# A value-and-output projection kernel: the first load in two halves by partitions, and four clips moved behind two casts

## The reference

```
q = cond @ Wq.T + bq;  k = x @ Wk.T + bk;  v = x @ Wv.T + bv
scores = q . k / sqrt(32) per head           # one number for each row of x and head
context = clip(scores, 0, 1) * v             # per head
out = x + context @ Wo.T + bo
```

## Time and profile before

| what | value |
|---|---|
| median of 3 runs | 178.35 us (177.8 to 178.4) |
| the profiled execution | 178.37 us |
| its span, first to last instruction | 176.5 us |
| TensorE busy | 171.7 us, 97% |
| VectorE busy | 158.1 us, 90% |
| ScalarE busy | 110.9 us, 63% |
| granted TensorE clock | 1.000 of full |
| transfers | 29.72 MB, 168 GB/s mean |

### The profile page before, as it was taken

One profiled execution on the slowest core, in us unless ns is written; L12 is line 12 of the kernel. 1 busy time (PEld: TensorE's weight loads), 2 busy tenths in 40 slices (PEclk: granted clock), 3 DMA queues, 4 the chain that ended last, 5 costly groups with the idle time before them and its releaser, 6 DMA issues.

```text
span 176.5 us, 2441 instructions
## 1 busy us (share of the span) xinstructions
PE 171.7 (97%) x859; PEld 134.7 (76%) x859; DVE 158.1 (90%) x163; ACT 110.9 (63%) x150; POOL 10.7 (6%) x16
## 2 busy tenths in 40 slices
PE   8899999999999899999999999999999999999993
PEld 2786857687788688888688888888688888888883
DVE  0798499989988899989998899999999999999963
ACT  3658697974588857583489765766299555684300
POOL 0000000000000020111000010111000010111000
PEclk9999999999999999999999999999999999999999
DMA  5999950079900589998006844297107024197544
GB/s 199 368 348 419 418 202 0 0 207 425 400 15 0 155 322 378 323 195 133 17 0 193 297 97 97 19 187 122 35 17 197 0 22 97 18 169 114 178 178 178
DMA packets 7307, 29.72 MB, mean 168 GB/s; under 512 B 1088, under 2 KB 1472, under 8 KB 6976
## 3 DMA queue, kind: packets, MB, share of 16 engines
q1 hardware_dynamic: 5568, 23.29, 36.2%
q0 software_dynamic: 1728, 6.29, 21.2%
HBM read 19.61 MB, written 14.68 MB: 194 GB/s over the span
## 4 chain that ended last, share of the span: by engine, by line
PE 95%; DMA 2%; issue 1%; ACT 0%; DVE 0%
PE bank_y L327 10%; PE bank_y L329 10%; PE bank_y L331 10%; PE bank_x L327 8%; PE bank_x L331 8%; PE bank_x L329 8%; PE bank_z L327 6%; PE bank_z L329 6%; PE bank_z L331 6%; PE bank_x L412 5%; PE score_bank L395 4%; PE bank_z L412 3%; DMA work<-first_t 2%; PE bank_x L430 2%; PE bank_y L430 2%; PE bank_y L412 2%
## 5 line engine op out<-in xcount | busy, mean ns | idle before, releaser
L553 ACT CAST form_hi<-work 128x1024 fp32r<-128x1024 f32 x28 | 28.9, 1053 | 16.6 <-DVE work L841 7.0
L796 DVE TENSOR_TENSOR form_lo<-work,form_hi 128x1024 fp32r<-128x1024 f32 (+1 forms) x30 | 35.0, 1185 | 2.5 <-ACT form_hi L553 2.5
L589 ACT ACTIVATE work<-bank_y,const 128x512 f32<-128x512 f32 x30 | 20.2, 688 | 14.7 <-PE bank_y L331 14.6
L327 PE MATMUL bank_x<-form_hi,wo_hi 128*128 128x512 f32 x52 | 20.4, 392 | 0.6 <-issue 0.6
L589 ACT ACTIVATE work<-bank_x,const 128x512 f32<-128x512 f32 x24 | 16.3, 688 | 6.7 <-PE bank_x L331 6.5
L331 PE MATMUL bank_x<-form_hi,wo_lo 128*128 128x512 f32 x52 | 20.3, 390 | 0.0
L329 PE MATMUL bank_x<-form_lo,wo_hi 128*128 128x512 f32 x52 | 20.2, 389 | 0.0
L782 POOL DMA_DIRECT2D out_t<-work x12 | 10.5, 875 | 149.8 <-DVE work L823 143.0
L812 DVE SCALAR_TENSOR_TENSOR work<-relu,work 128x1024 f32<-128x1024 f32 x16 | 19.3, 1219 | 0.0
L327 PE MATMUL bank_y<-form_hi,wv_hi 128*128 128x512 f32 x48 | 19.0, 397 | 0.0
L796 DVE TENSOR_TENSOR form_lo<-x_home,form_hi 128x1024 fp32r<-128x1024 f32 x15 | 18.3, 1219 | 0.6 <-ACT form_hi L620 0.6
(11 more groups left out here) (133 smaller groups left out, 343.3 us busy)
## 6 DMA issues: line engine op xcount, KB each, us to landing
x_home<-x_t SPq DMA_DIRECT2D x16, 512.0 KB, 7.0
out_t<-x_t SPq DMA_DIRECT2D x12, 512.0 KB, 8.3
out_t<-work POOLq DMA_DIRECT2D x12, 512.0 KB, 5.4
relu<-relu SPq DMA_DIRECT2D x12, 128.0 KB, 2.3
work<-first_t SPq DMA_DIRECT2D x2, 512.0 KB, 3.9
work<-wq_t SPq DMA_DIRECT2D x2, 512.0 KB, 8.9
work<-wk_t SPq DMA_DIRECT2D x2, 512.0 KB, 11.3
work<-wo_t SPq DMA_DIRECT2D x1, 1024.0 KB, 15.2
```

Of the source, the lines that this page charges most:

```text
L327: pe.matmul(bank[:, j, :], hi, form_hi[:, kind, k, :], start=k == 0 and not grows, stop=False, skip_group_check=grows)
L553: nc.scalar.copy(flat(form_hi, kind), raw(kind, phase)).then_inc(hi_ready[kind], 1)
L589: nc.scalar.activation(result_set(phase)[:, q, j * ROWS:(j + 1) * ROWS], of[:, j, :], ACT.Identity, bias=bias[:, tile:tile + 1], scale=sca ...
L796: return nc.vector.tensor_tensor(to, of, hi.bitcast(F32), ALU.subtract)
```

## The change

The load of the first tile (k = 0) is issued as two transfers of 64 partitions each: partitions 0 to 63 by SyncE, partitions 64 to 127 by ScalarE, as the first thing in ScalarE's list. Both raise `first_loaded[0]`, and all who wait for it now wait for 32. The load for k = 1 stays whole and SyncE's. Apart from that, `clip_scores(1)` is moved down in ScalarE's list past `hi(T2, 2)` and `hi(B22, 2)`.

```diff
+FIRST_LOADS = (2 * 16, 16)
...
-            for k in range(2):
-                sp.dma_start(work[1][:, k, :], first_t[k]).then_inc(first_loaded[k], 16)
+            sp.dma_start(work[1][0:P // 2, 0, :], first_t[0, 0:P // 2, :]).then_inc(first_loaded[0], 16)
+            sp.dma_start(work[1][:, 1, :], first_t[1]).then_inc(first_loaded[1], 16)
...
             def first_half(k, semaphore):
-                act.wait_ge(first_loaded[k], 16)
+                act.wait_ge(first_loaded[k], FIRST_LOADS[k])
...
+            act.dma_start(work[1][P // 2:P, 0, :], first_t[0, P // 2:P, :]).then_inc(first_loaded[0], 16)
             first_half(0, first_half_hi)
...
             hi(B11, 3)
-            clip_scores(1)
             hi(T2, 2)
             hi(B22, 2)
+            clip_scores(1)
             hi(B21, 3)
```

More of the change, by code:

```diff
@@ L941, in first_w_hi @@
             def first_w_hi(form, k):
-                dve.wait_ge(first_loaded[k], 16)
+                dve.wait_ge(first_loaded[k], FIRST_LOADS[k])
                 nc.vector.tensor_copy(wv_hi[:, form, k, :], first_w[form][:, k, :]).then_inc(wv_hi_ready[form], 1)
```

## The result

Over 22 runs the changed kernel has a median of 178.58 us (178.08 to 180.55), the kernel before 178.42 us (177.8 to 179.04) over as many. The ratio of after to before is 1.0044, 95% interval 1.0025 to 1.0063: a little slower. The medians hide what happened. The kernel before has one group of runs. The changed kernel has two: 12 of its 22 runs lie from 178.08 to 178.66, mean 178.36, and 10 from 179.76 to 180.55, mean 180.20. None of the 22 lies under the lowest run of the kernel before. The profiled execution is of the upper group, 180.55 us with a span of 178.7.

The account below looks back on a forecast made before the run. TensorE, busy for 97% of the span, was taken to bound the kernel. From 178.37 us, 0 for the split load and −0.71 for the moved clips gave 177.7 us, range 177.2 to 178.6.

Parts of the forecast that it names:

- The clips: ScalarE, phase 2: clips hold the cast of T2 for 1.2 us; moving them gains 0.71 us, at most 0.84.
- VectorE's add: VectorE, phase 2: this add, at 56.94, precedes T2's lo part, which would start at 58.08 instead of 58.79.
- the cast of T3: ScalarE, phase 2: ends at 62.4 instead of 62.23; 1.4 us of cover before TensorE needs T3's lo part, cost nothing.
- The margin at T2 of phase 4: Narrowest gap after the stall between a lo part's end and its product: 1.6 us, so the whole 0.71 should last.
- The first load: Kernel start: splitting it into partition halves was priced at 0, with 0.21 us won at best and 1.09 lost at worst.
- inner range of ±0.2: Kernel start: expected change of the first tile's landing, −0.2 to +0.2 us around 0, assuming something near the full rate.
- the bad end: Kernel start: both halves move at 221 GB/s throughout, so the first tile takes 2.37 us instead of 1.28, 1.09 later.
- the 221 GB/s of the spread: Rate of the clips' spreading over 32 partitions while alone, where full tiles moved 410; taken as the low-rate bound.
- My bound of +1.09: Kernel start: largest delay in us forecast for the first tile's landing, with both halves at 221 GB/s all through.
- The half-rate rival: Kernel start: halves move like the 32-partition spread or one starts an issue later; costs 0.2 to 1.09 us, 178.2 us; chance 0.26.
- The table load: ScalarE's start: forecast to move from 0.73 to about 1.2 at no cost; rival with it ahead: 178.9 us, chance 0.05.
- a later landing: Kernel start: a landing later or earlier by d moves TensorE's start by d, and nearly all follows to the end.

Follow-up runs that it names:

- the larger set of runs: Clips moved, first load whole on SyncE, against the kernel before, run a second time: median 177.70 us over 12 runs, ratio 0.9961; means 0.82 us apart.

## Why the prediction was wrong

The prediction was 177.7 us, 0.4% faster, with a range of 177.2 to 178.6. The median of 178.58 lies at its very edge, and the time moved the other way.

**The clips: right, by its mechanism and its size.** The stall was the clips' doing, and 0.71 us was forecast; the trace of this edit alone shows 0.72, and the larger set of runs 0.8. VectorE's add is the next thing late, as said. What was left is 0.04 us there and 0.08 in the changed kernel; the 0.08 by which T2's second matmul follows late stayed (59.09 to 59.40), so 0.76 and not 0.84 was the most to be had. Of the pushed work, the cast of T3 was forecast to leave 1.4 us of cover, and it leaves 1.4 (66.53 to 67.97). The margin at T2 of phase 4 stayed at 1.6, since VectorE moved along with TensorE.

**The first load: wrong, and this is the step that failed.** I took 0 with an inner range of ±0.2, on the ground that with both halves under way at once the other half fills in. It does not. TensorE's first product started 0.8 us later in one profile of the changed kernel and 1.5 in the other. The row that I had set as the bad end, the 221 GB/s of the spread, was the nearer one: 229 to 283 GB/s while halves are being moved. My bound of +1.09 was too small for two of the four profiles with a half in each queue: the last half landed at 5.02, 5.24, 5.53 and 5.74 instead of 4.24, so 0.8 to 1.5 us late. At the mean rates up to the landing, 210 GB/s against 299, the 0.82 MB of the kernel before would take 3.9 us instead of 2.74; this estimate gives 1.2 of the 1.5 us of the profiled run. One term that was not in the bound is the issue: a half's takes 0.57 and not 0.21 or 0.43, with or without a second queue. What the rest is made of isn't shown. The half-rate rival, to which I gave 0.26 and 178.2 us, is what happened, and at the upper end of its price or above. The table load did move behind the new issue, to 1.33, and costs nothing, as forecast.

**What I did not price at all: the clock.** I passed a later landing on to TensorE's start one to one. In 10 of 22 runs it came with 1.7 to 1.8 us more (the trace, and the two groups' means), as the idle before the first product grew from 0.5 to 1.75 us and the first eight matmuls ran at 1.2 GHz. The cover here is the nine warm-ups, and the trace of before had them in it. I had named what hides each edit, but not what the warm-ups hide. For the profiled run the terms are 178.37 + 1.5 (start) + 1.7 (clock) − 0.7 (T2) = 180.9, measured 180.55; 0.3 of the rest lies between the eleventh product and the last of B21, 51.55 us in this profile (10.57 to 62.12) and 51.83 in that of before (7.40 to 59.23). For the lower group, 178.38 (mean before) + 0.8 − 0.7 = 178.5, measured 178.36, with the 0.8 from a single profile of another set. That the median came so near the upper bound of my range, 178.6, is luck: it lies between two groups, and no run but one fell between 178.51 and 179.76.

**Open.** What decides in a given run whether the clock rises before the first product was not settled: after nine slow warm-ups an idle of 1.75 us was followed by eight slow matmuls, one of 1.83 by none. Only one run of an upper group was profiled, so that the slow matmuls make up the others too rests on the size of the gap and on the run with 14 warm-ups. Nor is it shown why half a tile's issue takes longer than a whole one's, or why the whole tile issued behind a half takes long too. Which half lands last differs by run: ScalarE's in one profile, SyncE's in three.

## What to carry to other kernels

Dividing this load by partitions brought the mean rate up to its landing from 299 GB/s (kernel before) down to 203 to 265 (five profiles, 203 with both halves in one queue); by columns it cost nothing and gained nothing. So leave such a load whole and first in its queue, ahead of everything that competes. A load on which TensorE's start depends had two prices here, the delay and the clock. Warm-up matmuls should reach near its landing (14 instead of 9 took the upper group away), and runs have to be looked at as a distribution and not as a median. And where an engine works through a list in order, look for what stands ahead of the one instruction that is late: moving four clips of the kernel before is worth 0.4% by itself, and no variant here was faster than that kernel, 177.5 to 177.7 us.

## What the runs showed of the hardware that was not expected

- A load to 64 partitions of 4 KB took 0.56 to 0.59 us to issue. The whole tiles of `first_t` took 0.38 to 0.43, but 0.57 to 0.81 where one stood behind such a half in SyncE's queue. SyncE's half took 3.5 us from issue to landing in two profiles, like the whole tile, and 4.3 to 5.0 in three.
- With the two partition halves in two queues the DMA engines read as fully busy (1.07, 1.10) at 279 and 229 GB/s; with column halves they read 1.08 at 424. Some of these bytes are of the tile k = 1.
- The granted clock read 1.00 in windows in which matmuls of 512 columns were 0.43 us apart. The spacing of the matmuls tells the level, the column doesn't.
- Nine warm-ups of 512 columns took from 3.43 to 4.00 us in different profiles, by whether the last of them were already quick. With 4.00, zero, about three or eight of the first products were slow.
